# Window attention with a sort beside it, a graph over sorted edges and four experts: keys masked by head on ScalarE, and the last fix-ups inside the edge stage

## The reference

```python
y  = x + shifted_attention(attention(norm(x)))   # both: 8x8 windows, 8 heads of 16, qkv 128->384, out 128->128
t  = norm(y).reshape(32768, 128)                 # tokens; second attention: shifted by 4, with a mask
h  = t @ W_gat                                   # (32768, 4 heads, 4 experts)
e  = leaky_relu(a_src[src] + a_dst[dst])         # 524288 edges and 32768 self-loops
alpha = softmax of e over the edges of one dst
agg   = segment_sum(h[src] * alpha, dst)
gate  = softmax of the two best of mean over heads of layernorm(agg)
out   = y + sum over 4 experts of gate * (gelu(t @ W1 + b1) @ W2 + b2)
```

## Time and profile before

| | us |
|---|---|
| median of three executions | 8224.57 (8219.5 to 8226.58) |
| profiled execution | 8225.16 |
| its span, first to last instruction | 8223.3 |
| attention | 0 to 2212 |
| edges | 2212 to 7743 |
| ends | 7743 to 7760 |
| combine | 7760 to 8223 |

### The profile page before, as it was taken

One profiled execution on the slowest core, in us unless ns is written; L12 is line 12 of the kernel. 1 busy time (PEld: TensorE's weight loads), 2 busy tenths in 40 slices (PEclk: granted clock), 3 DMA queues, 4 the chain that ended last, 5 costly groups with the idle time before them and its releaser, 6 DMA issues. The chain is left out here.

```text
span 8223.3 us, 105909 instructions
## 1 busy us (share of the span) xinstructions
PE 4280.7 (52%) x31501; PEld 2348.5 (29%) x31501; DVE 5088.4 (62%) x15628; ACT 2131.3 (26%) x3826; POOL 4854.7 (59%) x5216
## 2 busy tenths in 40 slices
PE   5888888888643544535445354453544535445200
PEld 3556656556411221212212122121221212212000
DVE  9998889888745545445455454554545445455378
ACT  4666767666300100101001001010100101101034
POOL 2221112111377777777777777777777777777572
PEclk8889999999765665655656556565565655656555
DMA  1111111111211111111111111111111111111267
GB/s 48 51 51 49 50 54 52 49 55 48 62 32 37 38 32 43 32 32 43 32 43 32 32 43 32 43 32 32 43 32 43 32 32 43 32 43 32 80 202 251
DMA packets 537640, 419.78 MB, mean 51 GB/s; under 512 B 177554, under 2 KB 450498, under 8 KB 536642
## 3 DMA queue, kind: packets, MB, share of 16 engines
q1 hardware_dynamic: 323058, 323.88, 11.8%
q0 software_dynamic: 147552, 56.96, 7.0%
q10 hardware_dynamic: 66560, 33.56, 1.4%
HBM read 203.65 MB, written 176.72 MB: 46 GB/s over the span
## 5 line engine op out<-in xcount | busy, mean ns | idle before, releaser
L1326 POOL DMA_INDIRECT edge_G<-node_rows,edge_src x4352 | 4161.1, 956 | 1326.3 <-issue 1326.3
L1363 PE MATMUL edge_cbank<-edge_ohh,edge_ohl 128*128 128x256 bf16 x4096 | 1418.2, 395 | 2951.9 <-DVE edge_ohh L1496 2876.5
L1363 PEld LDWEIGHTS edge_cbank<-edge_ohh,edge_ohl 128*128 128x128 bf16 x4096 | 426.3, 104 | 3937.2 <-DVE edge_ohh L1496 3762.3
L1496 DVE TENSOR_SCALAR edge_ohh<-edge_iob,edge_dlf 128x256 bf16<-128x256 bf16 x4096 | 1196.7, 298 | 0.0
L564 POOL TENSOR_SCALAR attn_nw<-attn_mv 128x8 f32<-128x8 f32 x64 | 86.4, 1350 | 1725.5 <-DVE attn_mv L993 1725.4
L1495 DVE TENSOR_SCALAR edge_ohl<-edge_iob,edge_dlf 128x128 bf16<-128x128 bf16 x4096 | 1087.0, 266 | 14.8 <-DVE edge_dlf L1489 14.5
L1343 ACT ACTIVATE edge_hid<-edge_hbank,edge_b1c 128x512 f32<-128x512 f32 x512 | 351.6, 687 | 2498.2 <-PE edge_hbank L1370 2498.2
L1454 DVE COPY edge_O<-edge_O 128x24 f32<-128x24 f32 x64 | 12.7, 198 | 1534.6 <-DMA edge_G<-node_rows,edge_src 1534.6
L1506 DVE TENSOR_TENSOR edge_yo<-edge_ybank,edge_b2r 128x512 f32<-128x512 f32 x256 | 176.9, 691 | 946.4 <-PE edge_ybank L1379 946.4
L1346 ACT ACTIVATE edge_w<-edge_w 128x272 f32<-128x272 f32 x64 | 27.5, 429 | 2407.0 <-DVE edge_w L1468 2407.0
L1370 PE MATMUL edge_hbank<-edge_xt,edge_w 128*128 128x512 f32 x1024 | 590.2, 726 | 0.4 <-ACT edge_hid L1343 0.4
(11 more groups left out here) (239 smaller groups left out, 6383.1 us busy)
## 6 DMA issues: line engine op xcount, KB each, us to landing
edge_G<-node_rows,edge_src POOLq DMA_INDIRECT x4352, 2.4
expert_out<-edge_yo SPq DMA_DIRECT2D x64, 1024.0 KB
comb_ye<-expert_out SPq DMA_DIRECT2D x32, 2048.0 KB, 12.0
state_rows<-edge_O SPq DMA_DIRECT2D x64, 816.0 KB, 4.2
attn_km<-attn_kT SPq DMA_DIRECT2D x2048, 16.0 KB, 1.8
attn_xin<-in_x SPq DMA_DIRECT2D x32, 512.0 KB, 4.2
attn_xres<-in_x SPq DMA_DIRECT2D x32, 512.0 KB, 5.3
x_rows<-attn_x SPq DMA_DIRECT2D x32, 512.0 KB, 3.1
```

Of the source, the lines that this page charges most:

```text
L1326: pool.indirect_dma_start(G[b][:, t, :], None, node_rows, bass.IndirectOffsetOnAxis(ap=src[b][:, t:t + 1], axis=0)).then_inc(s_g[b][2 * t ...
L1363: pe.matmul(cbank[b][:, 0:HI], ohl[:, t % RING, :], ohh[:, t % RING, :], start=(t == 0), stop=(t == HC - 1)).then_inc(s_ohp, 1)
L1496: dve.tensor_scalar(ohh[:, t % RING, :], iob[:, :], dlf[:, 1, t:t + 1], None, ALU.is_equal).then_inc(s_oh, 1)
```

## The change

In attention, `kT`, `own_rows`, its semaphores and the clearing of `km` go. `km` holds both halves of an image. ACT drains a key task with four ACTIVATEs instead of one, each over all 128 partitions and 512 columns, with a per-partition factor (`of_head`: 1 in the rows of head g and g + 4, else 0) and a per-partition bias (`kbias`). PE waits for the task's bank to be free instead of for the transfers. DVE makes `of_head` and `kbias` once at the start (seven small instructions).

In edges, SP loads the first keys ahead of the weights, DVE waits for nine constants of POOL instead of for the weights, and the ends stage is gone: its constants are made at the start of edges, its row numbers (`end_rows`) behind the last chunk's `outputs`, the carry over the partitions (`carried`) behind the last chunk's `math`, read straight from SBUF. POOL waits for all state stores before it gathers the old rows. `combine` reads the row numbers from SBUF.

```diff
-            def own_rows(s, m, q):
...
-                for head in range(HEADS):
-                    lo = head * HDIM
-                    sp.dma_start(km[st][lo:lo + HDIM, r, head % (HEADS // 2), :, :].rearrange("p w k -> p (w k)"),
-                                 kT[st][h][lo:lo + HDIM, c:c + QWIN * WTOK]).then_inc(s_km[st][r], 16)
...
+            def keys_by_head(n, task):
+                st, h, m = STREAM[task[0]], int(task[2]), n - LAG[task]
+                t, free = take(n, task)
+                if m > 0:
+                    act.wait_ge(s_sc, (m - 1 + LAG[task[0]]) * PAIRS + 4 * h + 4)
+                for g in range(HEADS // 2):
+                    last = act.activation(km[st][:, h, g, :, :].rearrange("p w k -> p (w k)"), t[:, :], ACT.Identity,
+                                          bias=kbias[:, g:g + 1], scale=of_head[:, g:g + 1])
+                last.then_inc(free, 1)
...
-                q = j // 2
-                if j % 2 == 0:
-                    pe.wait_ge(s_km[st][q % KRING], KM_DONE * (2 * m + q // 2 + 1))
+                    wait_free(pe, f"{s}k{h}", m)
...
-            dve.wait_ge(s_c, 2)
-            dve.wait_ge(s_w, 64)
+            dve.wait_ge(s_c, CONSTANTS)
...
+            load_keys(0, 0)
+            load_keys(1, 1)
+            load_raw(0, 0)
+            load_x(0, 0)
+            sp.dma_start(w1[:, :, :], W1.rearrange("e p f -> p e f")).then_inc(s_w, 16)
...
+                if last_of(b, i):
+                    end_rows()
                 st.k = 0
                 math(b, i, at + C)
                 assert st.k == M
+                if last_of(b, i):
+                    carried(O[b])
...
+            pool.wait_ge(s_end, mark["row"])
+            for b in range(2):
+                pool.wait_ge(s_st[b], 16 * CHUNKS // 2)
             pool.wait_ge(s_z, 16)
             pool.indirect_dma_start(old[:, :], None, state_rows, bass.IndirectOffsetOnAxis(ap=ri[:, 0:1], axis=0)).then_inc(s_old, 16)
...
-            sp.dma_start(ix[:, :], end_rows).then_inc(s_ix, 16)
...
-            pool.wait_ge(s_ix, 16)
```

More of the change, by code:

```diff
@@ L1201, in edges @@
         yo = [sb(f"yo{b}", [P, UTILES, EXPERTS * P]) for b in range(2)]
+        tri = sb("tri", [P, P])
+        ones = sb("ones", [P, P])
+        ident = sb("ident", [P, P])
+        rowi = sb("rowi", [P, HI], I32)
+        rowf = sb("rowf", [P, HI])
+        pref = sb("pref", [P, HI])
+        tot = sb("tot", [P, HI])
+        zero = sb("zero", [P, HI])
+        nost = sb("nost", [P, 1])
+        x3 = sb("x3", [P, 3, VCH])
+        xe = sb("xe", [VCH, 3, P])
+        most = sb("most", [VCH, P + 1])
+        total = sb("total", [VCH, P + 1])
+        w2e = sb("w2e", [VCH, 2, P])
+        car = sb("car", [P, 2, VCH])
+        old = sb("old", [P, NROW])
+        new = sb("new", [P, NROW])
+        mm = sb("mm", [P, VCH])
+        mo = sb("mo", [P, VCH])
+        wc = sb("wc", [P, 2, VCH])
+        has = sb("has", [P, 1])
+        ri = sb("ri", [P, 2], I32)
+        rf = sb("rf", [P, 4])
         hbank = [ps("hbank0"), ps("hbank1")]
@@ L1253, in edges @@
         block = ctx.enter_context(nc.Block())
[L1255 to L1330, removed]
@@ L1332, in _ @@
-        @block.scalar
-        def _(act):
-            act.wait_ge(s_w, 64)
-            def body(b, i):
-                c = 2 * i + b
-                for k in range(EXPERTS * HB):
-                    act.wait_ge(s_l1, c * EXPERTS * HB + k + 1)
-                    if k == 0 and not first_of(b, i):
-                        act.wait_ge(s_l2, c * UTILES)
-                    act.activation(hid[:, k, :], hbank[k % 2][:, :], ACT.Gelu, bias=b1c[:, k:k + 1]).then_inc(s_ge, 1)
-                act.wait_ge(s_lo, c + 1)
-                act.activation(w[:, 0, :, :], w[:, 0, :, :], ACT.Exp).then_inc(s_ex, 1)
-                act.activation(wbank[:, 0:GHEADS * TC].rearrange("p (h t) -> p h t", h=GHEADS), w[:, 1, :, :], ACT.Exp).then_inc(s_ex, 1)
-            chunks(act, body)
@@ L1679, in _, with body @@
             pool.iota(ri[:, 1:2], pattern=[[0, 1]], base=SORTED, channel_multiplier=1).then_inc(s_c, 1)
-            pool.wait_ge(s_step, mark["row"])
+            pool.wait_ge(s_dec, 1)
+            pool.indirect_dma_start(ad0[:, :], None, node_rows, bass.IndirectOffsetOnAxis(ap=first[:, :], axis=0)).then_inc(s_ad, 16)
+            def body(b, i):
+                c = 2 * i + b
+                pool.wait_ge(s_dec, c + 1)
+                if not first_of(b, i, 2):
+                    pool.wait_ge(s_math, c - 1)
+                pool.sem_inc(s_passed, 1)
+                for t in range(TC):
+                    pool.indirect_dma_start(G[b][:, t, :], None, node_rows,
+                                            bass.IndirectOffsetOnAxis(ap=src[b][:, t:t + 1], axis=0)
+                                            ).then_inc(s_g[b][2 * t // TC], 16)
@@ new lines, in _, with body @@
+        def _(act):
+            act.wait_ge(s_w, 64)
+            def body(b, i):
+                c = 2 * i + b
+                for k in range(EXPERTS * HB):
+                    act.wait_ge(s_l1, c * EXPERTS * HB + k + 1)
+                    if k == 0 and not first_of(b, i):
+                        act.wait_ge(s_l2, c * UTILES)
+                    act.activation(hid[:, k, :], hbank[k % 2][:, :], ACT.Gelu, bias=b1c[:, k:k + 1]).then_inc(s_ge, 1)
+                act.wait_ge(s_lo, c + 1)
+                act.activation(w[:, 0, :, :], w[:, 0, :, :], ACT.Exp).then_inc(s_ex, 1)
+                act.activation(wbank[:, 0:GHEADS * TC].rearrange("p (h t) -> p h t", h=GHEADS), w[:, 1, :, :], ACT.Exp).then_inc(s_ex, 1)
+            chunks(act, body)
+            act.wait_ge(s_end, mark["w2"])
+            act.activation(w2e[:, :, :], w2e[:, :, :], ACT.Exp).then_inc(s_act, 1)
+            act.wait_ge(s_end, mark["wc"])
+            act.activation(wc[:, :, :], wc[:, :, :], ACT.Exp).then_inc(s_act, 1)
@@ L1693, in _ @@
+            chunks(pe, body)
+            pe.wait_ge(s_hs, CHUNKS)
+            pe.wait_ge(s_c, CONSTANTS)
+            pe.matmul(hbank[0][:, 0:HI], tri[:, :], hist[:, :], start=True, stop=True)
+            pe.matmul(hbank[1][:, 0:HI], ones[:, :], hist[:, :], start=True, stop=True).then_inc(s_pe, 1)
+            pe.wait_ge(s_end, mark["x3"])
             for k in range(3):
-                last = pe.transpose(bx[0:VCH, k * P:(k + 1) * P], x3[:, k, :], ident[:, :])
+                last = pe.transpose(cbank[0][0:VCH, k * P:(k + 1) * P], x3[:, k, :], ident[:, :])
@@ L1708, in combine @@
[L1708 removed]
+            pe.wait_ge(s_end, mark["V"])
+            pe.transpose(cbank[1][:, 0:VCH], most[:, 0:P], ident[0:VCH, 0:VCH])
+            pe.transpose(cbank[1][:, VCH:2 * VCH], total[:, 0:P], ident[0:VCH, 0:VCH]).then_inc(s_pe, 1)
+def combine(nc, state_rows, ix, expert_out, x2_rows, b_gat, gamma, beta, out):
     SIZES = (8, 8, 8, 4, 4)
```

358 lines of the change are left out of this document (153 added, 205 removed).

## The result

The changed kernel takes 8354.5 us (median of 4 runs, 8350.6 to 8360.5), the kernel before on the same chip 8225.6. The ratio is 1.0154, with a 95% interval of 1.0136 to 1.0172: slower, by about 129 us, and 20 us above the top of the predicted range. The profiled execution spans 8348.9 us, 125.6 more than that of before.

What follows compares the result with a forecast made beforehand. Attention was taken as bound by DVE's fixed work plus its waits, edges by POOL's gathers. From 8225.2 us, +70 for attention's waits, -5 for the start of edges and -20 for the fold gave 8270, range 8195 to 8335.

Steps and rivals of the forecast that it cites:

- Transfers: Attention, slots 4 and 5: DVE's waits of 1.55 and 1.96 us go, gaining 3.5 us per step.
- Four ACTIVATEs: ACT's key drain in attention: 0.80 us each, 0.70 apart, four taking 2.9 us where one took 0.675.
- the cheap factor: Rival, ACT's key drains: the per-partition factor costs nothing, ACTIVATEs 0.565 us apart, say 8205 us; chance 0.15.
- Slot 2: Attention: scores behind `Aq1` and `Bq1` come late, DVE waits 3.3 us per step; 2.5 at full clock.
- Slot 5 and slot 6's scores: Attention: `CH0` waits for `Ak0`'s bank, scores behind it; DVE waits 0.6 us per step, bounds 0.2 and 1.5.
- `CZ`: Attention, slot 6: `CZ0` waits for `Bk0`'s bank; DVE's wait becomes 4.0 us per step, bounds 3.3 and 5.
- Sum: DVE's attention waits: 8.3 us per step against 5.95 before, 2.35 more in each of 30 steps, +70 us.
- Start of edges: Edge stage's start: keys load ahead of the weights, the first gather comes sooner; gain 5 us, bounds 4 and 6.
- Fold: Last state store to combine's first gather, 34.7 us before: gain 20 us, bounds 14 and 22.
- the clock falls every time: Rival, PE in attention: stops of slots 1, 5, 6 bring 1.2 GHz every step; 10.5 us per step, 8335; chance 0.17.
- that rival's 8095: Rival, attention: engines slide and only the transfers' waits go, 3.5 us per step gained, none lost; 8095 us; chance 0.13.

Runs made afterwards that it cites:

- the better order: Changed kernel with each key task last and alone in its slot (slots 1, 2, 4, 5), same work on every engine: 8111.1 us, ratio 0.9866 to the kernel before.

## Why the prediction failed

The mechanism and each of its places were right; the sizes at three of them were too small, by 2.5 us a step together. Point by point:

- *Transfers.* The waits of slots 4 and 5 went, 3.5 us a step, as forecast (1.55 and 1.96 to 0).
- *Four ACTIVATEs.* 0.80 us each and 2.9 for four; measured 0.775 and 2.76 to 2.78. The choice against the cheap factor was right (88 ns for the operand in the run with a constant factor). The Trainium skill (ScalarE: Activation LUTs, What ACT_TABLE_LOAD costs) gives about 93 ns for such an operand; the trace agrees with 88.
- *Slot 2.* Forecast 3.3, measured 4.02, inside the bounds. 2.5 was the sum with full clock, 4.0 to 4.5 with the half clock, and I took the middle. The half clock came in 23 of 26 steps.
- *Slot 5 and slot 6's scores.* Forecast 0.6, bounds 0.2 and 1.5, measured 1.64, above the bound. `CH0` waited 2.3 us as worked out (55.0 us over 24 times); what was missing is that the matmuls behind that stop, 16 of `CH0`, the sort's transposes and the scores, run at 1.2 GHz.
- *`CZ`.* Forecast 4.0, measured 4.63. I gave the clock 0.2 us. The slow stretch behind `CH0`'s stop makes PE late for `Bk0`: in the step shown the transposes ahead of it take 1.76 us in place of 1.09, and with the added matmuls the wait is 3.89. It is not the clock at `CZ0` itself, which was back at 2.4 GHz in all 25 of these stops; the half clock behind them falls on the scores of slot 7, for which DVE waits 0.05 us.
- *Sum.* Forecast 8.3 us a step, measured 10.82 with the small waits of slots 0 and 1 as before; 10.82 - 5.85 = 4.97 us, 149 us over 30 steps, where I had 70 (the stage's end moved by 146).
- *Start of edges.* -5 forecast, -5.3 measured.
- *Fold.* -20 forecast, -15.3 measured. The bound of 14 was named for the wrong cause: not a late completion of a store, but GpSimd's drain. The sum had 0.5 us for the barrier; from the landing of the rows' update (7881.7) to the first gather it took 8.3.

The step that failed is thus a choice in the sum: at each of the three places the half clock was weighed as something that comes now and then, with the one 4.39 us stop of the earlier trace rows as its only sight. The rest of the sum holds: with the added matmuls, which keep the clock up, DVE waited 2.34 us at slot 2 and 3.89 for `CZ`, where the prediction had 2.5 and 3.8 at full clock. The rival "the clock falls every time" put 10.5 us a step and 8335 us; the traces show 10.82, and its chance of 0.17 was too low. What spoke against it, that two of the stops are shorter than the one seen, was no argument: stops of 2.7 and 1.2 us in the mean brought it in slot 1 and of 2.3 us in slot 5, and in the run with two ACTIVATEs stops of 1.0 us brought it in 17 of 29 steps. The run with added matmuls gives the clock at least 100 of the 149 us; without it the time would have been near 8225 + 43 - 5 - 15 = 8248, under the forecast. The Trainium skill (TensorE: Matmul & The Clock Gate, HAM oscillation) describes an engine that cools down again at each wait of a loop. The trace agrees in the pattern, with the slow score groups counted above, but not in the size: the waits of the page's kernel are for transfers and longer than these stops, so by it alone this case would not have been foreseen. The 20 us between the range's top, which was this rival's time, and the median are 10 us in attention (146 for its 136), 5 in the fold and 4 by which the profiled execution lies under the median.

That the engines can slide once nothing stops them is true (the run with one ACTIVATE, 8045 us, is even under that rival's 8095). With all four ACTIVATEs and the key tasks last, attention gains 1.02 points (0.9968 to 0.9866), 84 us of the 154; the changed kernel lost them to the place in which the longer drain stood. Open is how the clock and the stops share the loss of each single place: the added matmuls stood at all four waits at once, and in slot 6 they left 10 of 27 score groups slow.

## What to carry to other kernels

A longer drain may cost little on its own engine, as here; ask which task takes that bank next, and put something else between. Where a stop of TensorE is new, work out the sum at half clock for everything behind it first, and take less only if a row shows the clock surviving such a stop. And when a small stage is folded into one with thousands of indirect transfers, look at what the engines do to meet at its end: that work may have been hidden.

## What the runs showed that I had not expected

- Added matmuls whose result nobody reads paid: four of 128x240 in front of each of four waits, 103 us gained with more work. In the better order the same step brought nothing, and 0.9 us more wait per step.
- GpSimd's drain at a stage's end ended 8.4 us after the last of the edge stage's gathers (before and in the run with the explicit drain), in the changed kernel 8.6 us after the rows' update although the gathers were 25 us old, and only 1.3 us after the update where two indirect transfers had gone before. An idle time of 20 us ahead of it did not shorten it; an explicit drain did. What it does in that time no run here tells.
- The price of the drain's length is steep near the point where the wait shows: 0.35 us less in each drain was worth some 78 us, in a single run.
